# Attention and bit-weight feed-forward on one core: values ahead of scores on PE, another order of DMA issues, and the weight sums split over POOL and DVE

## The chip, the cores and the metric

The kernel runs on one core of one Trainium2 chip. The metric is the device time in microseconds (us) of one execution; the change is judged against the kernel before, timed on the same chip.

## The reference, cut to what matters

Inputs `x` and `ctx_2048` are [4, 1024, 1024] f32. The block is a causal cross attention with 16 heads of 64 columns (the context is both key and value), followed by a feed-forward whose weights are made from two four-bit-plane tensors of [1024, 1024, 4].

```python
q = heads(_layernorm(x)); k = v = heads(ctx)                    # 16 heads of 64
out = softmax(causal(q @ k.T * 64**-0.5)) @ v
x = x + out
soft = sigmoid(pweight) - sigmoid(nweight)                      # [1024, 1024, 4]
weight = einsum('oin,n->oi', soft, exps * sigmoid(mask_weight)) * scale
bias = round-to-4-bits(einsum('on,n->o', pbias - nbias, bexps)) * biasscale
x = x + _layernorm(x) @ weight.T + bias
```

## The kernel before, in words

**Tiles and jobs.** The 4 x 1024 rows make 32 tiles t of 128 rows; i = t % 8 is the place in the batch, so that tile t sees i+1 blocks of 128 keys. A tile's 16 heads are cut into jobs: 4 jobs of 4 heads for i = 0 and 1, 8 jobs of 2 heads for i = 2 and 3, and 16 jobs of one head for i = 4 to 7 ("16-step tiles"; q is the job's number in its tile). There are 352 jobs, and every engine walks through the same list, one step for each job j, with its own work of the step written out by hand. Nothing is scheduled by a planner: the order on each engine is the order of the code, and semaphores join the engines.

**One job on the five engines.** `scores(j)` (PE, L401, L402, L405) makes the scores of the job in one of two PSUM places (`slot`), as a sum of products in half precision, with the mask added by a last matmul. `maxima(j)` (DVE, L636) takes the row maxima, `exponentials(j)` (ACT, L520) writes exp to `p32`. `transpose_p(j)` (PE, L415) turns the 128 x 128 blocks of it into PSUM (`ptb`, two chunks), ACT writes the f16 high part (`high_parts`, L536) and DVE the f16 rest (`low_parts`, L642), and `values(j)` (PE, L434 and L436) multiplies both with the values into `oacc`. When four heads are done, ACT copies `oacc` to `osb` (`output`, L543), and POOL adds it to the row (`add_attention`, L867 to L876). PE fills each step with a piece of the feed-forward of an earlier tile (`linear`, L452).

**Turned jobs.** In tiles with one or two heads per job, jobs with q = 3, 6, 9, 12, 15 skip the transposes on PE. ACT writes the high part in place (L529, `p16`), DVE the low part (`low_part_unturned`, L650), and SP issues one DMA transpose (`turn_p`, L308) into `ptd`, from which `values(j)` reads. There are 92 such jobs.

**Distance.** In step j, PE does `scores` of job j+2, `values` of job j-2, the transposes of job j, and a piece of `linear`. DVE does in step j: `maxima(j+2)`, `low_part_unturned(j+1)` if job j+1 is turned, `low_parts(j)`, and the rest. So the scores of j+2 come in step j, the DMA transpose of j+1 is issued after it, and the values of j+1 are due three steps later.

**SP's list.** SP (SyncE) issues all DMAs in one written order: `turn_p`; `load_x` and `load_c` (rows and context of tile t+3); `turn_k`, `turn_q` (transposes of keys and queries of tile t+2, L296, L302); `swap_q` (two copies that make `qs`, L315, L316, which need `turn_q` landed); `turn_y`; `store`. A step number in SP's loop only sets the place in the list: SP goes on as soon as the semaphores that an issue waits for allow it.

**The weights.** Steps 0 to 15 (tiles 0 to 2) also make the feed-forward's weights, one unit u of two chunks w = 2u, 2u+1 per step: ACT takes tanh of both halves of each chunk (`chunk_tanh`, L582). For the even chunk DVE subtracts (L704), multiplies with the coefficients (L707) and sums over the four bits (L710); for the odd one POOL subtracts (`difference`, L883), and PE sums it with diagonal matrices (L475). PE turns both into `ffnb`, ACT (L576) and DVE (L715) split them into `wt`, and only then may PE begin the next unit.

## Time and profile before

| | us |
|---|---|
| median of three timed runs (1245.62 to 1248.9) | 1247.53 |
| the profiled execution's own time | 1242.35 |
| its span, first to last instruction | 1240.6 |
| PE busy in the span | 1114.4 (90%) |
| DVE busy | 1020.3 (82%) |
| ACT busy | 927.0 (75%) |
| POOL busy | 692.6 (56%) |

The granted TensorE clock is 0.975 of full speed over the span. PE's share is that of matmuls whose ends are modelled, and it averages over stages: up to about 170 us the weights are made beside the first jobs, then come the remaining tiles.

### The profile page before, as it was taken

How to read it: one execution, taken by the hardware profiler on the slowest of the kernel's cores; microseconds unless marked ns; L12 is line 12 of the kernel's file. 1: busy time of each engine (PE TensorE's matmuls, PEld its weight loads, DVE VectorE, ACT ScalarE, POOL GpSimd, SP SyncE). 2: the span in 40 equal slices, each digit the busy share in tenths (PEclk: the TensorE clock that was granted, in tenths of full speed). 3: DMA queues.
4: the chain of work that ended last, by engine and by line, in shares of the span. 5: the costliest groups of instructions: out<-in, count | busy, mean ns of one | idle time of the engine just before them, and what ended most of it. 6: DMA issues, size and time to landing. Idle time of an engine off the chain costs nothing. (4 is left out here: it accounts for less than half of the span.)

```text
span 1240.6 us, 28237 instructions
## 1 busy us (share of the span) xinstructions
PE 1114.4 (90%) x10820; PEld 813.7 (66%) x10820; DVE 1020.3 (82%) x1456; ACT 927.0 (75%) x1930; POOL 692.6 (56%) x766
## 2 busy tenths in 40 slices
PE   3687889989998999899998999899998998899988
PEld 2676756666766766666665777676776676676663
DVE  6989986888897887788897887888987887888862
ACT  5798975787887787777777787688787787787750
POOL 2456555554545886554445886554447986362351
PEclk8798999999999999999999999999999999999999
DMA  9699944756657888665667787576659886565442
GB/s 311 206 301 308 318 76 105 141 132 122 146 112 163 178 159 171 134 137 104 138 125 167 161 180 157 128 150 121 139 103 196 168 181 142 125 117 89 90 86 68
DMA packets 387189, 190.88 MB, mean 154 GB/s; under 512 B 358640, under 2 KB 358640, under 8 KB 387056
## 3 DMA queue, kind: packets, MB, share of 16 engines
q1 hardware_dynamic: 386048, 189.05, 67.7%
q8 instruction: 86, 1.41, 0.5%
q14 instruction: 47, 0.39, 0.1%
q10 hardware_dynamic: 1008, 0.04, 0.0%
HBM read 67.15 MB, written 16.78 MB: 68 GB/s over the span
## 5 line engine op out<-in xcount | busy, mean ns | idle before, releaser
L520 ACT ACTIVATE p<-slot,mx 128x512 f32<-128x512 f32 (+7 forms) x512 | 377.7, 746 | 151.7 <-DVE mx L636 94.2
L636 DVE TENSOR_REDUCE mx<-slot 128x1 f32<-128x640 f32 (+7 forms) x352 | 356.5, 1015 | 42.4 <-PE slot L405 40.5
L452 PE MATMUL ffnb<-wt,yt 128*128 128x512 f16 x1464 | 374.5, 382 | 3.1 <-DVE ring L698 1.7
L642 DVE SCALAR_TENSOR_TENSOR pt<-ptb,pt 128x512 f16<-128x512 f32 (+1 forms) x504 | 281.3, 598 | 100.4 <-ACT pt L536 100.3
L401 PE MATMUL slot<-kt,qt 128*128 128x128 f16 (+3 forms) x1056 | 269.5, 285 | 23.5 <-ACT p L520 11.3
L402 PE MATMUL slot<-kt,qs 128*128 128x128 f16 (+3 forms) x1056 | 268.8, 284 | 0.0
L536 ACT ACTIVATE pt<-ptb 128x512 f16<-128x512 f32 (+1 forms) x504 | 239.4, 527 | 31.9 <-PE ptb L415 30.7
L867 POOL TENSOR_TENSOR att<-osb 128x256 f32<-128x256 f32 x128 | 100.2, 783 | 289.2 <-ACT osb L543 282.8
L415 PE MATMUL ptb<-id,p 128*128 128x128 f32 x1700 | 240.3, 280 | 11.7 <-DVE pt L642 10.5
L452 PEld LDWEIGHTS ffnb<-wt,yt 128*128 128x128 f16 x1464 | 137.4, 99 | 104.3 <-issue 4.8
L434 PE MATMUL oacc<-v,pt 128*128 128x128 f16 x1700 | 180.4, 220 | 23.8 <-ACT osb L543 10.9
L415 PEld LDWEIGHTS ptb<-id,p 128*128 128x128 f32 x1700 | 182.1, 141 | 18.9 <-issue 15.9
L434 PEld LDWEIGHTS oacc<-v,pt 128*128 128x128 f16 x1700 | 150.4, 98 | 45.5 <-ACT osb L543 19.3
L436 PE MATMUL oacc<-v,pt 128*128 128x64 f16 x1700 | 173.0, 193 | 0.0
L401 PEld LDWEIGHTS slot<-kt,qt 128*128 128x128 f16 x1056 | 105.1, 100 | 100.9 <-ACT p L520 31.8
L650 DVE SCALAR_TENSOR_TENSOR p<-p 128x640 f16<-128x640 f32 (+3 forms) x92 | 138.4, 1505 | 19.7 <-ACT p L529 17.7
L436 PEld LDWEIGHTS oacc<-v,pt 128*128 128x128 f16 x1700 | 148.1, 98 | 0.1
L402 PEld LDWEIGHTS slot<-kt,qs 128*128 128x128 f16 x1056 | 104.3, 99 | 52.2 <-issue 0.7
L543 ACT ACTIVATE osb<-oacc 128x512 f32<-128x512 f32 x128 | 76.4, 597 | 53.3 <-PE oacc L436 53.0
L876 POOL TENSOR_TENSOR ring<-ring,att 128x256 f32<-128x256 f32 x128 | 105.6, 825 | 10.1
L405 PE MATMUL slot<-maskb,idb 128*128 128x128 bf16 x512 | 111.2, 221 | 0.0
L520 ACT ACTIVATION_READ_ACCUMULATOR p<-slot,mx 128x1 f32 x512 | 106.9, 209 | 0.0
(96 smaller groups left out, 1517.1 us busy)
## 6 DMA issues: line engine op xcount, KB each, us to landing
ring<-in_x_dram SPq DMA_DIRECT2D x32, 512.0 KB, 4.7
cin<-in_ctx_dram SPq DMA_DIRECT2D x32, 512.0 KB, 4.0
out_dram<-ring SPq DMA_DIRECT2D x32, 512.0 KB, 3.4
qs<-qt SPq DMA_DIRECT2D x124, 128.0 KB, 2.8
v<-in_L_ffn_pweight_dram SPq DMA_DIRECT2D x22, 512.0 KB, 6.7
kt<-in_L_ffn_nweight_dram SPq DMA_DIRECT2D x16, 512.0 KB, 7.6
v<-in_L_ffn_nweight_dram SPq DMA_DIRECT2D x6, 512.0 KB, 6.3
kt<-in_L_ffn_pweight_dram SPq DMA_DIRECT2D x5, 512.0 KB, 4.8
```

The costliest lines, as they stand in the source:

```text
L401: pe.matmul(dst, qt[:, t % 2, h, :], keys, start=True, stop=False, skip_group_check=True)
L402: last = pe.matmul(dst, qs[:, h, :], keys, start=False, stop=end <= i, skip_group_check=True)
L405: last = pe.matmul(slot[:, j.par, base + i * P:base + (i + 1) * P], idb[:, :], maskb[:, :], start=False, stop=True, skip_group_check=True)
L415: last = pe.transpose(ptb[:, c % 2, at * P:(at + 1) * P], p32[:, j.par, k * P:(k + 1) * P], id32[:, :])
L434: pe.matmul(oacc[:, h % GROUP, :], turned[:, k, :], v, start=blk == 0, stop=False, skip_group_check=True)
L436: last = pe.matmul(oacc[:, h % GROUP, 0:D], turned[:, j.blocks + k, :], v[:, 0:D], start=False, stop=blk == j.i, skip_group_check=True)
L452: last = pe.matmul(dst, yt[:, k % 2, a * KT_N + kk, :], wt[:, c, kk, half * 512:half * 512 + 512], start=r == 0, stop=r == 3 * KT_N - 1)
L520: last = nc.scalar.activation(p32[:, j.par, hh * j.keys:(hh + 1) * j.keys], slot[:, j.par, base:base + j.keys], ACT.Exp, bias=mx[:, j.par, ...
L536: nc.scalar.activation(pt[:, j.par, blocks.start:blocks.stop, :], ptb[:, c % 2, 0:P * len(blocks)].rearrange("p (k c) -> p k c", c=P), ACT ...
L636: nc.vector.tensor_reduce(mx[:, j.par, 0:j.heads], src[:, 0:j.heads, 0:j.keys], AX_X, ALU.max, negate=True).then_inc(mx_ready, 1)
L642: nc.vector.scalar_tensor_tensor(pt[:, j.par, j.blocks + blocks.start:j.blocks + blocks.stop, :], ptb[:, c % 2, 0:P * len(blocks)].rearran ...
L650: nc.vector.scalar_tensor_tensor(p16[:, size:2 * size], p32[:, j.par, 0:size], P_SCALE, p16[:, 0:size], ALU.mult, ALU.subtract).then_inc(p ...
```

## The change

1. On PE, `values` of the job two back stands ahead of `scores` of the job two on, in every step.
2. On SP, in 16-step tiles: `load_x` and `load_c` both at step 9 (they were at 8 and 7), `turn_k` at 12 (was 9), `turn_q` at 14, which is behind `turn_p(15)` as before, but ahead of `turn_k` in the last tile of a batch. `LOADS` leaves the other tiles as they were.
3. The sum over the four bits on DVE: one multiplication and three multiply-adds on 256 elements, each with a stride of four in its source, take the place of one multiplication and one reduction on 1024. The subtraction ahead of it goes to POOL for every second unit (`on_pool`).

```diff
+LOADS = {4: (2, 2), 8: (4, 4), 16: (9, 9)}
...
+def on_pool(w):
+    return w % 4 != 2
+def differences_to(w):
+    return sum(on_pool(v) for v in range(w + 1))
 def turn_k_step(t):
-    return 9 if steps(t) == 16 and t % NT < NT - 1 else steps(t) - 1
+    return 12 if steps(t) == 16 and t % NT < NT - 1 else steps(t) - 1
...
# SP
+                    if s == 14 and n == 16 and t + 2 < TILES:
+                        turn_q(t + 2)
-                    if s == n // 2 and t + 3 < TILES:
+                    if s == LOADS[n][0] and t + 3 < TILES:
                         load_x(t + 3)
-                    if s == C_LO[n] + n // 16 and t + 3 < TILES:
+                    if s == LOADS[n][1] and t + 3 < TILES:
                         load_c(t + 3)
...
-                    if s == n - 1 and t + 2 < TILES:
+                    if s == n - 1 and n < 16 and t + 2 < TILES:
                         turn_q(t + 2)
# PE
-                pe.wait_ge(d_ready, u + 1)
+                pe.wait_ge(d_ready, differences_to(2 * u + 1))
...
             for j in JOBS:
+                if j.n > 1:
+                    values(JOBS[j.n - 2])
                 if j.n + 2 < len(JOBS):
                     scores(JOBS[j.n + 2])
-                if j.n > 1:
-                    values(JOBS[j.n - 2])
                 transpose_p(j)
# DVE, weights_sum(u): before
-                dve.wait_ge(th_ready, w + 1)
-                nc.vector.tensor_tensor(pairs[w % PAIRS][0], pairs[w % PAIRS][0], pairs[w % PAIRS][1], ALU.subtract
-                                        ).then_inc(w_sub, 1)
-                nc.vector.tensor_tensor(a, a, coef.unsqueeze(1).to_broadcast([P, WCH, NBITS]), ALU.mult
-                                        ).then_inc(w_mul, 1)
-                nc.vector.tensor_reduce(pairs[w % PAIRS][1][:, 0:WCH], a, AX_X, ALU.add).then_inc(w_sum, 1)
# DVE, weights_sum(u): now
+                if u % 2:
+                    dve.wait_ge(th_ready, w + 1)
+                    nc.vector.tensor_tensor(d, d, c, ALU.subtract).then_inc(w_sub, 1)
+                    dve.wait_ge(w_sub, u // 2 + 1)
+                else:
+                    dve.wait_ge(d_ready, differences_to(w))
+                nc.vector.tensor_scalar(acc, bit[:, :, 0], coef[:, 0:1], None, ALU.mult).then_inc(w_mul, 1)
+                nc.vector.scalar_tensor_tensor(acc, bit[:, :, 1], coef[:, 1:2], acc, ALU.mult, ALU.add
+                                               ).then_inc(w_mul, 1)
...
# POOL
+                if j.n + 1 < UNITS and on_pool(2 * j.n + 2):
+                    difference(2 * j.n + 2)
                 if j.n > 1 and JOBS[j.n - 2].closes_group:
                     add_attention(JOBS[j.n - 2].group)
                 if j.n + 1 < UNITS:
-                    difference(j.n + 1)
+                    difference(2 * j.n + 3)
```

PE, tile 4 (one head, five key blocks), the first turned job, whose values read `ptd`. Before:

```order
L405 MATMUL slot<-maskb,idb 128x128
L434 MATMUL oacc<-v16,ptd 128x128
L436 MATMUL oacc<-v16,ptd 128x64
L434 MATMUL oacc<-v16,ptd 128x128
L436 MATMUL oacc<-v16,ptd 128x64
L434 MATMUL oacc<-v16,ptd 128x128
L436 MATMUL oacc<-v16,ptd 128x64
L434 MATMUL oacc<-v16,ptd 128x128
L436 MATMUL oacc<-v16,ptd 128x64
L434 MATMUL oacc<-v16,ptd 128x128
L436 MATMUL oacc<-v16,ptd 128x64
L415 MATMUL ptb<-id32,p32 128x128 x5
```

And of the change (L466 is `linear`, L448 and L450 `values`, L415 the scores with `kt16`):

```order
L466 MATMUL ffnb<-wt,yt 128x512 x4
L448 MATMUL oacc<-v16,ptd 128x128
L450 MATMUL oacc<-v16,ptd 128x64
L448 MATMUL oacc<-v16,ptd 128x128
L450 MATMUL oacc<-v16,ptd 128x64
L448 MATMUL oacc<-v16,ptd 128x128
L450 MATMUL oacc<-v16,ptd 128x64
L448 MATMUL oacc<-v16,ptd 128x128
L450 MATMUL oacc<-v16,ptd 128x64
L448 MATMUL oacc<-v16,ptd 128x128
L450 MATMUL oacc<-v16,ptd 128x64
L415 MATMUL slot<-kt16,qt 128x512
```

The values stood between the scores' last matmul and the transposes; they stand between `linear` and the scores' first matmul now.

SP, the last tile of a batch (tile 7), from `turn_p` of its job 6. Before:

```order
L308 DMA_TRANSPOSE ptd<-p 128x16x128
L315 DMA qs<-qt 64x1024
L316 DMA qs<-qt 64x1024
L283 DMA cin<-in_ctx_dram 128x1024
L308 DMA_TRANSPOSE ptd<-p 128x16x128
L279 DMA ring<-in_x_dram 128x1024
L308 DMA_TRANSPOSE ptd<-p 128x16x128
L315 DMA qs<-qt 64x1024
L316 DMA qs<-qt 64x1024
L308 DMA_TRANSPOSE ptd<-p 128x16x128
L296 DMA_TRANSPOSE kt<-v 128x16x128
L302 DMA_TRANSPOSE qt<-q 128x16x128
```

And of the change (L320 is `turn_p`, L291 `load_x`, L295 `load_c`, L314 `turn_q`, L308 `turn_k`, L327 and L328 `swap_q`):

```order
L320 DMA_TRANSPOSE ptd<-p 128x16x128
L327 DMA qs<-qt 64x1024
L328 DMA qs<-qt 64x1024
L320 DMA_TRANSPOSE ptd<-p 128x16x128
L291 DMA ring<-in_x_dram 128x1024
L295 DMA cin<-in_ctx_dram 128x1024
L320 DMA_TRANSPOSE ptd<-p 128x16x128
L327 DMA qs<-qt 64x1024
L328 DMA qs<-qt 64x1024
L320 DMA_TRANSPOSE ptd<-p 128x16x128
L314 DMA_TRANSPOSE qt<-q 128x16x128
L308 DMA_TRANSPOSE kt<-v 128x16x128
```

The context's load went from ahead of the second `turn_p` shown to behind it, and `turn_q` and `turn_k` changed places.

DVE, a unit of the weights whose subtraction goes to POOL (u = 6). Before:

```order
L642 SCALAR_TENSOR_TENSOR pt<-ptb,pt 128x512 [waits hi_done] x2
L704 TENSOR_TENSOR v16<-v16 128x1024 [waits w_tanh]
L707 TENSOR_TENSOR v16<-v16,small 128x1024 [waits w_sub]
L710 TENSOR_REDUCE v16<-v16 128x256 [waits w_mul]
L715 TENSOR_TENSOR wt<-ffnb,wt 128x4x128 [waits w_hi]
```

And of the change (L656 is `low_parts`, L739 `weights_low`; `w_diff` is POOL's semaphore `d_ready`):

```order
L656 SCALAR_TENSOR_TENSOR pt<-ptb,pt 128x512 [waits hi_done] x2
L725 TENSOR_SCALAR v16<-v16,small 128x256 [waits w_diff]
L727 SCALAR_TENSOR_TENSOR v16<-v16,small 128x256 [waits w_mul]
L730 SCALAR_TENSOR_TENSOR v16<-v16,small 128x256 [waits w_mul]
L733 SCALAR_TENSOR_TENSOR v16<-v16,small 128x256 [waits w_mul]
L739 TENSOR_TENSOR wt<-ffnb,wt 128x4x128 [waits w_hi]
```

Three instructions on 1024 elements gave way to four on 256, and the wait is for POOL's subtraction and not for ACT's tanh.

## Rows read from the trace of the kernel before

**Rows 1.** Busy time by stage: us, then PE, PEld, DVE, ACT, POOL, clock, DMA.
```profile
31.00:155.00 124.00, 94.35 (x635) 86.57 (x634) 114.54 (x139) 105.14 (x197) 68.54 (x56) 0.87 0.88 283
...
172.00:1216.00 1044.00, 975.60 (x9897) 697.60 (x9896) 868.18 (x1270) 793.69 (x1684) 607.53 (x678) 0.99 0.67 137
```

**Rows 2.** PE's waits, 172 to 1216 us: who for whom, us, times, longest.
```profile
PE oacc L434 <- DMA ptd<-p: 16.1, 15, 2.3
...
PE slot L401 <- issue: 9.8, 3, 3.8
PE oacc L434 <- DVE pt L642: 9.4, 15, 1.3
```

**Rows 3.** Timeline of tile 21 (six key blocks), a turned job: start, us, engine.
```profile
816.48 0.27 PE L401 MATMUL slot<-kt,qt 128*128 128x256 f16 x1
817.05 2.13 POOL L848 TENSOR_TENSOR v<-cin,v 128x1024 f16<-128x1024 f32 x1
817.19 0.22 PE L434 MATMUL oacc<-v,ptd 128*128 128x128 f16 x1
817.70 0.85 PE L415 MATMUL ptb<-id,p 128*128 128x128 f32 x6
817.82 0.95 DVE L636 TENSOR_REDUCE mx<-slot 128x1 f32<-128x768 f32 x1
818.69 1.31 DVE L650 SCALAR_TENSOR_TENSOR p<-p 128x768 f16<-128x768 f32 x1
820.02 1.72 SPq L308 DMA_TRANSPOSE ptd<-p  x1
824.63 0.23 PE L434 MATMUL oacc<-v,ptd 128*128 128x128 f16 x1 [0.29 <-DMA ptd<-p]
```

**Rows 4.** All DMA transposes of turned jobs (L308), by source line.
```profile
DMA to landing us min/median/max: 3.3/4.3/6.1
```

**Rows 5.** Stretches of tiles 20, 21, 22 and 23, columns as in rows 1.
```profile
747.32:788.29 40.97, 37.03 (x410) 28.47 (x408) 32.55 (x57) 29.71 (x68) 26.34 (x28) 1.00 0.72 152
788.29:830.91 42.62, 39.02 (x411) 29.81 (x411) 36.00 (x56) 33.33 (x69) 22.43 (x25) 1.00 0.68 136
830.91:876.04 45.13, 42.26 (x453) 32.45 (x452) 39.02 (x56) 36.01 (x67) 22.24 (x25) 1.00 0.69 133
876.04:924.57 48.53, 47.06 (x496) 34.80 (x494) 44.34 (x55) 38.22 (x65) 20.69 (x24) 1.00 0.59 116
```

**Rows 6.** DVE by form and by source line: count, busy us, mean ns; or min/median/max.
```profile
L636 DVE TENSOR_REDUCE mx<-slot 128x1 f32<-128x1024 f32 x64 | 77.1, 1209 | 2.0 <-PE slot L405 1.6
L642 DVE SCALAR_TENSOR_TENSOR pt<-ptb,pt 128x256 f16<-128x256 f32 x44 | 18.2, 413 | 0.0
L650 DVE SCALAR_TENSOR_TENSOR p<-p x92: 824/1226/2756, 212.7 to 1197.2; 128x768 f16<-128x768 f32 x26, 128x1024 f16<-128x1024 f32 x26, 128x640 f16<-128x640 f32 x20, 128x896 f16<-128x896 f32 x20
```

**Rows 7.** Timeline of SP and PE as batch 1 begins (tile 9's scores at 393.73).
```profile
382.57 3.66 SPq L296 DMA_TRANSPOSE kt<-v  x1
386.33 2.23 SPq L302 DMA_TRANSPOSE qt<-q  x1
390.72 0.46 SPq L315 DMA_DIRECT2D qs<-qt  x1
...
393.73 0.22 PE L401 MATMUL slot<-kt,qt 128*128 128x128 f16 x1 [3.00 <-issue]
```

**Rows 8.** DVE and POOL in the weights' stage, timeline; two stretches.
```profile
43.05 2.36 POOL L883 TENSOR_TENSOR v<-v,yt 128x1024 f32<-128x1024 f32 x1 [6.01 <-ACT yt L582]
43.38 2.08 DVE L727 TENSOR_TENSOR y<-y 128x32 f32<-128x32 f32 x1
...
80.49 1.37 DVE L704 TENSOR_TENSOR v<-v 128x1024 f32<-128x1024 f32 x1
81.89 1.23 DVE L707 TENSOR_TENSOR v<-v,small 128x1024 f32<-128x1024 f32 x1
83.15 1.22 DVE L710 TENSOR_REDUCE v<-v 128x256 f32<-128x1024 f32 x1
```

More of the change, by code:

```diff
@@ L701, in weights_sum @@
                 w = 2 * u
-                a = pairs[w % PAIRS][0].rearrange("p (k n) -> p k n", n=NBITS)
-                dve.wait_ge(th_ready, w + 1)
-                nc.vector.tensor_tensor(pairs[w % PAIRS][0], pairs[w % PAIRS][0], pairs[w % PAIRS][1], ALU.subtract
-                                        ).then_inc(w_sub, 1)
-                dve.wait_ge(w_sub, u + 1)
-                nc.vector.tensor_tensor(a, a, coef.unsqueeze(1).to_broadcast([P, WCH, NBITS]), ALU.mult
-                                        ).then_inc(w_mul, 1)
-                dve.wait_ge(w_mul, u + 1)
-                nc.vector.tensor_reduce(pairs[w % PAIRS][1][:, 0:WCH], a, AX_X, ALU.add).then_inc(w_sum, 1)
+                d, c = pairs[w % PAIRS]
+                if u % 2:
[4 more added lines that the diff above has]
+                    dve.wait_ge(d_ready, differences_to(w))
+                bit = d.rearrange("p (k n) -> p k n", n=NBITS)
+                acc = c[:, 0:WCH]
+                nc.vector.tensor_scalar(acc, bit[:, :, 0], coef[:, 0:1], None, ALU.mult).then_inc(w_mul, 1)
+                dve.wait_ge(w_mul, 3 * u + 1)
+                nc.vector.scalar_tensor_tensor(acc, bit[:, :, 1], coef[:, 1:2], acc, ALU.mult, ALU.add
+                                               ).then_inc(w_mul, 1)
+                dve.wait_ge(w_mul, 3 * u + 2)
+                nc.vector.scalar_tensor_tensor(acc, bit[:, :, 2], coef[:, 2:3], acc, ALU.mult, ALU.add
+                                               ).then_inc(w_mul, 1)
+                dve.wait_ge(w_mul, 3 * u + 3)
+                nc.vector.scalar_tensor_tensor(acc, bit[:, :, 3], coef[:, 3:4], acc, ALU.mult, ALU.add
+                                               ).then_inc(w_sum, 1)
             def weights_low(u):
@@ L877, in add_attention, with difference @@
                                         ).then_inc(x1_ready, 1)
-            def difference(u):
-                w = 2 * u + 1
+            def difference(w):
                 pool.wait_ge(th_ready, w + 1)
@@ L900, in _ @@
             difference(0)
+            difference(1)
             made, q_made = 0, 2
```

## The prediction

> **What bounds the kernel now.** I read the busy time by stage first [rows 1]. From 172 to 1216 us PE is busy 975.6 of 1044 us (93%), DVE 83%, ACT 76%: PE is the bound of this stage, and a stall of PE there costs its full length unless it takes the place of another. Before it, from 31 to 155 us, DVE is the fullest (114.5 of 124 us), ACT comes next (105.1) and PE has 94.4. That is the stage in which the weights are made; it is bound by DVE, with ACT close behind, and PE waits there.
>
> Then PE's waits in the long stage [rows 2]. The largest is for `ptd`, the DMA transpose of a turned job: 16.1 us in 15 waits. 92 jobs are turned, so most come in time now; the question is by how much. The timeline of one such job shows it [rows 3]. In one step of tile 21, PE starts the scores of job j+2 at 816.48, the values of the turned job before at 817.19, the transposes at 817.70. DVE takes the maxima of these scores from 817.82 to 818.77, then the low part of turned job j+1, 818.69 to 820.00 (it began while POOL's subtraction of 817.05 to 819.18 ran), SP issues its transpose at 820.02, and PE begins the values of j+1 at 824.63, after a wait of 0.29 us for it. From the scores' last matmul to these values the way is full: maxima, low part, DMA.
>
> **The change on PE.** It removes and adds no instruction on PE; it exchanges two blocks. Take `transpose_p(j)` and `linear` as fixed. The scores end later by the length of the values: 817.70 - 817.19 = 0.51 us with six blocks [rows 3]. The values are due earlier by the length of the scores: 817.19 - 816.48 = 0.71 us. So the way "scores of j+2 end, maxima, low part of j+1, DMA, values of j+1" has 0.51 + 0.71 = 1.22 us less. What stands on it after the change is a loop: the values of the last turned job (0.51), the scores (0.71, and 0.15 till the last matmul ends), maxima 0.95, low part 1.23 (the median [rows 6]), issue to landing 4.3 (the median [rows 4]), and about 0.2 for four handovers (an estimate; from DVE's end to SP's start it is 0.02 [rows 3]), together 8.05 us; then the next turned job's values, and so round. The loop spans three steps. Three steps of tile 21 take 42.62 x 3/16 = 7.99 us now [rows 5]. The same sum for the other widths (values and scores by 0.085 and 0.11 us per block, an estimate from the six-block lengths; maxima 0.8 to 1.21 [rows 6]) gives 7.7 for tile 20, 8.4 for 22 and 8.8 for 23, against 7.68, 8.46 and 9.10 now. So with median durations the loop is as long as PE's own work: half of the loops will be longer than it. A late loop costs PE its lateness, an early one gives nothing back, as PE can't run ahead of its own work. The low part lies between 0.82 and 2.76 us, the landing between 3.3 and 6.1: I take a spread of 0.8 us (one standard deviation) around a mean excess near 0.1. The mean of the positive part of that is 0.37 us, and 92 turned jobs make **+34 us**. Both ends: 0.12 us per job if the late low parts are late for POOL's sake and not for the scores' (then they don't move), +11; 0.6 if also the low parts of the turned-on-PE jobs come late, +55. For those speaks that PE waits 9.4 us in 15 waits for `pt` already [rows 2], and that DVE now does the maxima at the same time as PE the transposes, ahead of `low_parts`. What the exchange gives: the values cover a late exp at the step's start. That wait is below the ones shown in rows 2, under 9.4 us in all, and is inside the lengths that I compared with.
>
> **The change on SP.** In the last tile of a batch, `turn_k` (3.66 us to issue) stands ahead of `turn_q`, `turn_q` is issued at 386.33, and `swap_q`, which needs it landed, at 390.72; PE then waits 3.0 us with the first scores of tile 9, to 393.73 [rows 7]. Three batches do this, 9.8 us in all [rows 2]. With `turn_q` first it starts 3.66 us sooner; `swap_q` then stands behind `turn_k`'s issue, at about 382.6 + 2.2 + 3.7 = 388.5, which is 2.2 us sooner: **-7 us** over three batches (ends: -10, the whole wait, and 0, if the keys' transpose, now last, is the one missed). `load_c` no longer goes out just ahead of `turn_p(9)`. In tile 21, where it did, the transpose at 820.02 had not landed for the values at 824.63, 4.6 us later [rows 3]. I give 0.3 us to each of 16 such jobs, **-5 us** (ends 0 and -11). `turn_k` now follows `turn_p(12)` in place of `turn_p(9)`; both have a step or more till the next turn_p, and tile t+2's keys are due a tile later, so I cost it at nothing. Were SP late behind it, the turned job 15 would pay up to its 3.66 us of issue.
>
> **The change in the weights' stage.** DVE gives up for each unit a multiplication (1.23) and a reduction (1.22), and for eight of sixteen units a subtraction (1.37) [rows 8]. It gets one multiplication and three multiply-adds on 256 elements. Their price isn't in the trace; the nearest row is a multiply-subtract on 256 elements out of PSUM, 0.41 us [rows 6]. Bounds: 0.3 us (it scales down from 0.82 for 640 elements) and 1.2, if each waits for one POOL instruction. With 0.41 a sum is 1.65 and not 2.45 us: 16 x 0.8 + 8 x 1.37 = 24 us less for DVE. But ACT is busy 105.1 of the 124 us [rows 1] and has none of its work taken, so no more than 18.9 us can come out, and the chain "PE makes the unit, ACT and DVE split it, PE begins the next" stays. The moved subtraction takes 2.36 us on POOL for 1.37, DVE waits for it with `weights_low` and `maxima` queued behind, and POOL does `add_attention` after it. I take **-8 us** (ends 0 and -18.9).
>
> Here a rule speaks against the change. The row: a subtraction of 32 elements on DVE (L727) took 2.08 us, from 43.38 to 45.46, as long as POOL's subtraction of 43.05 to 45.41 ran [rows 8]. DVE's instructions with two SBUF sources wait for POOL's. The Trainium skill ("SBUF — State Buffer", Who interferes with whom) states this as a lock that is held for the whole instruction; by that rule, the trace agrees. Each multiply-add has two SBUF sources, and POOL gets eight more subtractions, so each sum may stand behind one; that is why I take less than half of the 18.9 us.
>
> The Trainium skill ("Vector Engine (DVE) Microarchitecture Reference", Points that are easy to get wrong) also says that this form of instruction runs at half rate with two SBUF sources that aren't bf16. The row L650 has f32 and f16 sources, and its 640 elements took 0.82 us at best [rows 6], 1.29 ns each, as little as the subtraction on 1024 elements with its 1.34 ns [rows 8]. That is the second rival below.
>
> **Sum.** +34 - 7 - 5 - 8 = +14 us on the profiled execution's 1242.35, 1256.4. That execution is 5.2 us under the median of the timed runs, so I forecast 1261.5, say **1262 us**.
>
> **Rivals.**
> 1. *The transposes are hidden anyway; the change is faster.* Place: the values of turned jobs. For it: only 15 of 92 wait now, and in many loops DVE reaches the low part late because of POOL, not because of the scores, so that 0.51 of the 1.22 us doesn't count. Against: tile 21's rows show nothing spare. With 0.12 us per job (+11), -7 - 5 - 12 beside it: -13, 1234 us. It decides from 0.22 us per turned job down, where +20 meets the three gains of 20. Chance 0.15.
> 2. *Multiply-adds at half rate.* Each takes 0.53 + 0.15 and not 0.41, 48 of them +13 us of DVE's 24 saved; with the wait for POOL's subtraction the stage gives nothing: +22, 1270. Chance 0.05; the row speaks against it.
> 3. *Two waits add up.* In the step after a turned job there are no transposes, so the low parts of the job ahead of it are due first, and turned values after them. If both slip, each loop is longer by the 1.22 us less what is spare, about 0.75: +69 - 12 - 8 = +49, 1297. For it: `pt` waits of rows 2. Chance 0.13.
> 4. *It cancels:* loss and gains each near 20, no change. Chance 0.09.
> My forecast's case has 0.58.
>
> **Numbers.** About 0.3% (3.7 us) is what a measurement of this kernel can tell from no change. The range takes the forecast's case from +20 to +45 for PE (1241 with gains of 26, 1280 with 12), rival 2, and half of rival 3; it leaves out most of rival 1: 1241 to 1290. Faster 0.17 (rival 1 and a little of the forecast's case), same 0.10, slower 0.73.
>
> **What would show it.** Right: PE's wait for `ptd` grows from 16 us to 40 or more, in over 40 waits; three steps of tile 20 and 21 become longer by 0.3 to 0.6 us; the wait of PE at the first scores of tiles 9, 17, 25 shrinks from 3.3 to about 1; L704 counts 8; the last unit of the weights is done some 8 us sooner; the new multiply-adds last 0.35 to 0.5 us apart from those that stand behind POOL. DVE's wait for ACT's `pt` falls, since maxima fill that time. Wrong: no more waits for `ptd` than now would take down the main term; multiply-adds of 0.7 us the third; the weights' stage not shorter, with ACT or POOL waiting in DVE's place, the same.

## The result and the profile after

The changed kernel takes 1276.07 us (median of four runs, 1274.9 to 1276.88) against 1246.74 of four runs of the kernel before beside it: ratio **1.0245**, 95% interval 1.0217 to 1.0273. It is slower, by 30 us. Here and below, each ratio is to the kernel before, timed beside the run on the same chip, with its 95% interval in brackets; differences are (ratio - 1) x 1246 us, and the interval of one is 1.5 to 5 us to either side. The texts on record write some of them as differences of the medians (+31.5 for +32.6, -15.4 for -15.0, +10.7 for +11.1). The lines of code named here moved by 12 to 24: L448 and L450 are the values, L415 and L416 the scores, L557 the copy of the finished group on ACT (`osb`), L650 the maxima, L656 `low_parts`, L664 the low part for a DMA transpose, L906 POOL's subtraction, L725, L727, L730 and L733 the new sum.

Busy time by stage, columns as in [rows 1]:

```profile
31.00:155.00 124.00, 86.49 (x557) 79.98 (x556) 106.53 (x143) 95.98 (x178) 75.03 (x57) 0.83 0.83 261
188.00:1250.00 1062.00, 966.35 (x9900) 683.87 (x9901) 871.05 (x1272) 796.70 (x1685) 604.51 (x678) 1.00 0.64 135
```

PE did less of its work in the first 124 us (557 matmuls where 635 were), and the long stage needs 1062 us for the matmuls that took 1044. The net loss of the two profiled executions has two places of about equal size. The last unit of the weights shows the first: `weights_low` (L739) of unit 16 starts at 183.5 us, and it started at 166.7 before.

```profile
L739 DVE TENSOR_TENSOR wt<-ffnb,wt x16: 636/677/692, 38.3 to 183.5; 128x512 f16<-128x512 f32 x16
```

PE's waits in the long stage, 188 to 1250 us, after:

```profile
PE oacc L448 <- ACT osb L557: 35.2, 42, 2.2
PE oacc L448 <- DVE pt L656: 31.3, 33, 1.6
PE oacc L448 <- DMA ptd<-p: 18.8, 29, 2.4
PE ptb L429 <- DVE pt L656: 5.5, 14, 2.1
PE slot L415 <- DMA qs<-qt: 1.4, 1, 1.4
```

and three rows of the same view of the kernel before (172 to 1216 us) that did not stand in [rows 2]:

```profile
PE oacc L434 <- ACT osb L543: 10.9, 21, 0.9
PE ptb L415 <- DVE pt L642: 10.5, 22, 2.0
...
PE slot L401 <- ACT p L520: 5.6, 15, 0.6
```

Three waits stand at the first matmul of the values. Together they were 36.4 us (16.1 and 9.4 of [rows 2], and 10.9) and are 85.3. The wait for the DMA transpose, on which the prediction built, grew least: 16.1 us in 15 waits to 18.8 in 29. What fell are the waits at the scores, 9.8 us at the batches' starts to under 2 and the one for exp, 5.6 us in 15 waits, to none, and the wait at the transposes (`ptb`), 10.5 us to 5.5.

Tiles 20, 21 and 22, to be read against [rows 5]:

```profile
769.94:809.76 39.82, 36.39 (x406) 27.64 (x404) 31.24 (x57) 30.78 (x69) 27.16 (x30) 1.00 0.70 148
809.76:854.49 44.73, 38.51 (x416) 29.17 (x414) 36.88 (x56) 32.50 (x67) 21.20 (x25) 1.00 0.59 126
854.49:903.09 48.60, 42.55 (x458) 31.74 (x456) 40.48 (x55) 36.04 (x67) 21.25 (x25) 1.00 0.63 123
```

Tile 20 became 1.2 us shorter, tiles 21 and 22 longer by 2.1 and 3.5: three steps of tile 21 take 8.39 us instead of 7.99.

Tile 21's turned job after, timeline (start, us, engine), to be read against [rows 3]:

```profile
838.94 0.96 DVE L650 TENSOR_REDUCE mx<-slot 128x1 f32<-128x768 f32 x1 [0.25 <-PE slot L419]
839.81 0.95 DVE L664 SCALAR_TENSOR_TENSOR p<-p 128x768 f16<-128x768 f32 x1
840.79 1.43 SPq L320 DMA_TRANSPOSE ptd<-p  x1
840.97 1.05 ACT L566 CAST q<-norm 128x1024 f16<-128x1024 f32 x1
841.90 0.61 ACT L557 ACTIVATE osb<-oacc 128x512 f32<-128x512 f32 x1
842.57 0.23 PE L448 MATMUL oacc<-v,pt 128*128 128x128 f16 x1 [0.49 <-ACT osb L557]
845.11 0.22 PE L448 MATMUL oacc<-v,ptd 128*128 128x128 f16 x1
```

The way from the maxima's start to the turned values is 6.17 us (838.94 to 845.11); it was 6.81 (817.82 to 824.63), and this transpose is in time, since the values one job ahead of it already stood for 0.49 us until ACT had copied `oacc`. ACT's list had a cast of 1.05 us ahead of that copy. DVE in turn waits for PE's scores more, 121.7 us in 139 waits of the long stage where it was 40.5 in 55.

One unit of the weights after, its subtraction now on POOL, timeline, to be read against [rows 8]:

```profile
83.42 2.35 POOL L906 TENSOR_TENSOR v<-v 128x1024 f32<-128x1024 f32 x1 [5.56 <-ACT v L596]
85.81 0.92 DVE L725 TENSOR_SCALAR v<-v,small 128x256 f32<-128x256 f32 x1 [3.63 <-POOL v L906]
86.77 0.84 DVE L727 SCALAR_TENSOR_TENSOR v<-v,small 128x256 f32<-128x256 f32 x1
87.64 0.90 DVE L730 SCALAR_TENSOR_TENSOR v<-v,small 128x256 f32<-128x256 f32 x1
88.11 2.60 POOL L906 TENSOR_TENSOR v<-v,kt 128x1024 f32<-128x1024 f32 x1
88.58 2.53 DVE L733 SCALAR_TENSOR_TENSOR v<-v,small 128x256 f32<-128x256 f32 x1
91.03 0.67 DVE L739 TENSOR_TENSOR wt<-ffnb,wt 128x512 f16<-128x512 f32 x1
```

DVE stands 3.63 us for POOL's subtraction, its multiply-adds take 0.84 and 0.90 us, and the last one, issued 0.47 us after POOL's next subtraction, takes 2.53. It ends at 91.11, 0.40 us behind POOL's subtraction (90.71), 1.9 us later than its own work would; `weights_low`, for which PE waits, is queued behind. Min/median/max of the last of the new lines in the `v` chunks (six of its sixteen instructions), where the median already is a wait for POOL:

```profile
L733 DVE SCALAR_TENSOR_TENSOR v<-v,small x6: 671/2516/2542, 29.8 to 173.8; 128x256 f32<-128x256 f32 x6
```

### The profile page after: what moved, and what is told of

Same layout as the page of the kernel before. It is cut to its first block, busy times and chain, and to the rows that moved or that the text cites. A ratio compares the mean times of both kernels' runs of the same rounds, so it can differ in the third digit from the quotient of the medians.

```text
span 1274.9 us, 28269 instructions
## 1 busy us (share of the span) xinstructions
PE 1110.3 (87%) x10820; PEld 804.9 (63%) x10820; DVE 1029.5 (81%) x1480; ACT 930.1 (73%) x1930; POOL 708.9 (56%) x774
## 4 chain that ended last, share of the span: by engine, by line
PE 37%; DVE 25%; DMA 14%; ACT 10%; issue 7%; POOL 6%; SPq 0%; POOLq 0%; ACTq 0%
DMA ptd<-p 13%; PE ffnb L466 11%; DVE p L664 8%; DVE mx L650 5%; PE oacc L448 5%; PE ptb L429 5%; PE slot L415 5%; PE slot L416 5%; DVE pt L656 4%; DVE stats L677 2%; ACT p L534 2%; PE oacc L450 2%; ACT pt L550 2%; POOL norm L849 2%; ACT osb L557 2%
## 5 line engine op out<-in xcount | busy, mean ns | idle before, releaser
L650 DVE TENSOR_REDUCE mx<-slot 128x1 f32<-128x640 f32 (+7 forms) x352 | 358.4, 1018 | 126.2 <-PE slot L419 124.5
L466 PE MATMUL ffnb<-wt,yt 128*128 128x512 f16 x1464 | 372.8, 381 | 2.0 <-DVE ring L712 1.1
L656 DVE SCALAR_TENSOR_TENSOR pt<-ptb,pt 128x512 f16<-128x512 f32 (+1 forms) x504 | 281.0, 597 | 48.4 <-ACT pt L550 45.9
L415 PE MATMUL slot<-kt,qt 128*128 128x128 f16 (+3 forms) x1056 | 270.5, 286 | 9.9 <-ACT p L534 6.2
L416 PE MATMUL slot<-kt,qs 128*128 128x128 f16 (+3 forms) x1056 | 270.1, 285 | 0.0
L448 PE MATMUL oacc<-v,pt 128*128 128x128 f16 x1700 | 184.2, 223 | 72.6 <-ACT osb L557 35.2
L429 PE MATMUL ptb<-id,p 128*128 128x128 f32 x1700 | 233.8, 276 | 5.6 <-DVE pt L656 5.5
L448 PEld LDWEIGHTS oacc<-v,pt 128*128 128x128 f16 x1700 | 152.9, 100 | 133.1 <-ACT osb L557 61.6
L466 PEld LDWEIGHTS ffnb<-wt,yt 128*128 128x128 f16 x1464 | 139.6, 98 | 105.5 <-issue 2.5
L450 PE MATMUL oacc<-v,pt 128*128 128x64 f16 x1700 | 176.2, 195 | 0.0
L450 PEld LDWEIGHTS oacc<-v,pt 128*128 128x128 f16 x1700 | 150.2, 99 | 18.0 <-issue 0.3
L664 DVE SCALAR_TENSOR_TENSOR p<-p 128x640 f16<-128x640 f32 (+3 forms) x92 | 138.3, 1503 | 4.7 <-ACT p L543 3.1
L415 PEld LDWEIGHTS slot<-kt,qt 128*128 128x128 f16 x1056 | 103.6, 99 | 33.6 <-ACT p L534 6.4
L416 PEld LDWEIGHTS slot<-kt,qs 128*128 128x128 f16 x1056 | 104.6, 99 | 18.9 <-issue 0.3
L894 POOL TENSOR_TENSOR att<-att,rinv 128x256 f32<-128x256 f32 x128 | 85.6, 669 | 24.6 <-DVE rinv L671 15.4
```

The lines of the kernel that those rows point to most:

```text
L415: pe.matmul(dst, qt[:, t % 2, h, :], keys, start=True, stop=False, skip_group_check=True)
L416: last = pe.matmul(dst, qs[:, h, :], keys, start=False, stop=end <= i, skip_group_check=True)
L429: last = pe.transpose(ptb[:, c % 2, at * P:(at + 1) * P], p32[:, j.par, k * P:(k + 1) * P], id32[:, :])
L448: pe.matmul(oacc[:, h % GROUP, :], turned[:, k, :], v, start=blk == 0, stop=False, skip_group_check=True)
L450: last = pe.matmul(oacc[:, h % GROUP, 0:D], turned[:, j.blocks + k, :], v[:, 0:D], start=False, stop=blk == j.i, skip_group_check=True)
L466: last = pe.matmul(dst, yt[:, k % 2, a * KT_N + kk, :], wt[:, c, kk, half * 512:half * 512 + 512], start=r == 0, stop=r == 3 * KT_N - 1)
```

## The experiments

### The three parts, one at a time

**TensorE's order alone.** The kernel before with these lines:

```diff
+                if j.n > 1:
+                    values(JOBS[j.n - 2])
                 if j.n + 2 < len(JOBS):
                     scores(JOBS[j.n + 2])
-                if j.n > 1:
-                    values(JOBS[j.n - 2])
```

> The kernel before with only PE's order changed (values of the job two back ahead of the scores). Theory A (the values are due earlier while ACT's, DVE's and SP's queues stay tied to the transposes, so all three waits at the values grow): +17 to +27 us, PE's waits at the values near 85 us in sum against 36, and the wait of the scores for exp gone. Rival B (the whole loss is from the weights' stage): within 5 us of before.

1.0262 (1.0233 to 1.0290), +32.6 us: above Theory A's +17 to +27, with the waits that it named, 90.5 us at the values, and none left for exp. Its waits at the values, 176 to 1250 us:

```profile
PE oacc L434 <- ACT osb L543: 35.1, 43, 2.2
PE oacc L434 <- DVE pt L642: 31.5, 35, 1.6
PE oacc L434 <- DMA ptd<-p: 23.9, 27, 2.3
```

**SyncE's order alone.** `LOADS`, `turn_k` at 12, `turn_q` at 14 as in the diff of the change, nothing else.

> The kernel before with only SP's list changed. Forecast's terms: -7 us where batches begin and -5 us for the turned job 9, so -12. If the gain is only where batches begin: -5 to -7, with the three waits of PE at the first scores of tiles 9, 17 and 25 (9.8 us) down to under 3.

0.9880 (0.9847 to 0.9913), -15.0 us: faster than both kernels, and near the -12. The three waits at the batches' starts fell from 9.8 to 4.4 us, not to under 3.

**The weights' part alone.** The sums and the subtractions as changed, both lists as before.

> The kernel before with only the weight sums changed (the multiply-adds, and every second subtraction on POOL). Theory A (multiply-adds at 0.68 us and standing behind POOL's subtraction make the stage longer by themselves): +10 to +17 us, all of it before tile 3. Rival B (they lose only together with PE's new order): within 4 us of before. The forecast had -8.

1.0089 (1.0058 to 1.0119), +11.1 us, inside Theory A's range. The last unit starts 11.8 us later.

The three add to +28.7 us against +30.5 measured together, the same within their intervals. Two more kernels take one part back out of the changed one. **The changed kernel with the old sums and subtractions:**

> The changed kernel with the weights' part undone: SyncE's and TensorE's orders as changed, sums and subtractions as before. If the parts add (+31.5 - 15.4): +16 us against before, about 1.013; if the orders of the two lists feed each other, under +10 or over +22. The prediction's own sum without its -8 was +22.

1.0169 (1.0138 to 1.0199), +21.1, above the +16 and short of the 22 that would have spoken for a feedback. **The changed kernel with PE's old order** (the diff above, reversed):

> The changed kernel with TensorE's order undone. If the parts add (-15.4 + 10.7): -5 us against before, about 0.996.

0.9979 (0.9967 to 0.9991), -2.6. So in the changed kernel the weights' part costs 30.5 - 21.1 = 9.4 us, PE's order 33.1, and SP's order, from +32.6 to +21.1, gives back 11.5 where it gave 15.0 alone. Each of these carries an interval of 3 to 5 us, so 11.5 and 15.0 can't be told apart, nor 9.4 and 11.1.

### The weights: which part, and why

**The sums alone**, all even subtractions on DVE as before (shortened; the last line stands for three, n = 1, 2, 3):

```diff
-    nc.vector.tensor_tensor(a, a, coef..., ALU.mult)
-    nc.vector.tensor_reduce(pairs[w % PAIRS][1][:, 0:WCH], a, AX_X, ALU.add)
+    nc.vector.tensor_scalar(acc, bit[:, :, 0], coef[:, 0:1], None, ALU.mult)
+    nc.vector.scalar_tensor_tensor(acc, bit[:, :, n], coef[:, n:n + 1], acc, ALU.mult, ALU.add)
```

> The kernel before with one edit: each sum of four on VectorE is one TENSOR_SCALAR and three multiply-adds instead of a product over 1,024 and a reduction; all its subtractions stay on VectorE. The product and reduction of before take 1.26 + 1.31 = 2.57 us a unit; the four new ones should take, by the trace of the changed kernel, 0.47 + 3 x 0.69 = 2.54 us with GpSimd idle, and about 2.2 to 2.5 us for each that stands behind a subtraction on GpSimd. Theory (the multiply-adds save nothing and queue behind GpSimd): the same or slower, +0 to +8 us against before. Rival (they save time and the moved subtraction is what costs the +10.7 us of the weights' part alone): -4 to -10 us.

1.0119 (1.0082 to 1.0157), +14.8 us, more than either answer gave, and the opposite of the rival's saving. **The moved subtraction alone**, product and reduction as before:

```diff
+    if u % 2:
         nc.vector.tensor_tensor(d, d, c, ALU.subtract)
+    else:
+        dve.wait_ge(d_ready, differences_to(w))
```

> The kernel before with one edit: GpSimd also takes the even subtraction of every second unit; product and reduction as before. Theory A (the multiply-adds are what costs): the subtraction moved saves VectorE 1.26 us in 16 units and costs GpSimd 2.35 us each, -3 to +3 us against before. Theory B (GpSimd's longer queue, with VectorE's sums waiting for it, costs most of the +10.7 us): +6 to +11 us.

1.0021 (1.0007 to 1.0035), +2.6 us: Theory A's answer, at its upper end. DVE's sixteen sums with their subtractions, added up over their lines in the traces: 63.7 us before, 54.5 with the subtraction moved, 95.1 with the new sums, 82.5 with both, 79.3 in the changed kernel. The new sum, not the move, is what costs. At their shortest in these traces old and new sum take the same: 1.22 + 1.22 = 2.44 us, and 0.45 + 0.67 + 0.68 + 0.67 = 2.46. In the run with the sums alone 27 of the 64 new instructions began while an instruction of POOL ran; these 27 took 32.7 us more than their shortest, the other 37 together 0.5 us more. In the changed kernel it is 33 of 64, with 29.3 us, and 0.4 us for the rest. So it is POOL, and hardly anything else, that makes the new sums long; how much of DVE's longer list reaches the end (31.4 us on DVE, 14.8 in the time) is not followed further. The moved work came back as a wait, 7.1 + 5.9 + 3.7 us (31 to 188 us of that run; one row):

```profile
DVE v L722 <- POOL v L897: 7.1, 2, 3.6
```

**The forms by themselves**, six of each on DVE alone, first with POOL idle; no part of the reference is computed:

> No part of the reference's work: DVE alone does six of each form on f32 and f16 data, first with POOL idle, then with POOL in a chain of subtractions on 1024 elements. Theory A (a multiply-add with two f32 SBUF sources runs at half rate, whatever the stride): 256 elements 0.68 us with stride 4, contiguous, and with an immediate; 1024 elements 2.3 us; 0.41 us if one source is f16 or in PSUM. Rival B (the stride of four costs it): contiguous 0.41 us, stride 4 0.68 us, and the same for an addition with stride 4. With POOL busy, forms with two SBUF sources take up to 2.4 us more, the reduction nothing.

The timeline's rows (start, us of all six): L68 multiply-add over 256 with stride 4, L70 contiguous, L78 its first source in PSUM, L80 over 1024, L84 an addition over 1024, L86 and L88 TENSOR_SCALAR with stride 4 and contiguous.

```profile
11.13 4.17 DVE L68 SCALAR_TENSOR_TENSOR acc<-four,coef,acc 128x256 f32<-128x256 f32 x6
15.33 3.09 DVE L70 SCALAR_TENSOR_TENSOR acc<-four,coef,acc 128x256 f32<-128x256 f32 x6
...
28.54 3.08 DVE L78 SCALAR_TENSOR_TENSOR acc<-bank,coef,acc 128x256 f32<-128x256 f32 x6
31.65 7.89 DVE L80 SCALAR_TENSOR_TENSOR acc<-four,coef,acc 128x1024 f32<-128x1024 f32 x6
...
43.41 7.53 DVE L84 TENSOR_TENSOR acc<-four,acc 128x1024 f32<-128x1024 f32 x6
50.97 2.85 DVE L86 TENSOR_SCALAR acc<-four,coef 128x256 f32<-128x256 f32 x6
53.86 2.29 DVE L88 TENSOR_SCALAR acc<-four,coef 128x256 f32<-128x256 f32 x6
```

The stride of four f32 makes 0.515 us, with the handover to the next instruction, into 0.695, which is what the rival said of the stride. Two f32 sources in SBUF cost nothing beside one in PSUM (3.09 and 3.08), and 1024 elements take 1.31 us, 5% more than the addition: no half rate, and Theory A is out.

**The same forms while POOL runs 90 subtractions**, line numbers one higher:

> Forms of VectorE alone, six of each, while GpSimd runs a chain of subtractions over 1,024; nothing of the reference is computed. With GpSimd idle they took 0.695 us (multiply-add over 256, stride 4), 0.475 (TENSOR_SCALAR, stride 4), 0.38 (contiguous), 0.633 (addition, stride 4), 1.255 (addition over 1,024), 1.315 (multiply-add over 1,024), 1.25 (reduction). If only forms with two sources in SBUF wait for a whole instruction of GpSimd: TENSOR_SCALAR and the reduction keep their time, the additions rise above 2 us. If TENSOR_SCALAR waits too (two of four stood at 2.5 us in some units of the run with four of them): it rises to about 2.4 us.

```profile
L81 DVE SCALAR_TENSOR_TENSOR acc<-four,coef,acc 128x1024 f32<-128x1024 f32 x6 | 18.8, 3128 | 0.2
...
L71 DVE SCALAR_TENSOR_TENSOR acc<-four,coef,acc 128x256 f32<-128x256 f32 x6 | 14.6, 2436 | 0.2
L87 DVE TENSOR_SCALAR acc<-four,coef 128x256 f32<-128x256 f32 x6 | 14.5, 2413 | 0.2
...
L91 DVE TENSOR_REDUCE acc<-four 128x256 f32<-128x1024 f32 x6 | 7.3, 1220 | 0.2
L79 DVE SCALAR_TENSOR_TENSOR acc<-bank,coef,acc 128x256 f32<-128x256 f32 x6 | 2.9, 484 | 0.2
...
L94 DVE COPY res<-src 128x4 f32<-128x4 f32 x1 | 2.2, 2185 | 0.0
```

TENSOR_SCALAR waits too, so the second answer of the expectation holds: each such instruction of 256 elements or fewer takes about as long as one subtraction of POOL (a copy of four elements 2.19 us). The reduction and the form that reads PSUM don't wait. So the old sum had one instruction that could stand behind POOL, its product; the reduction, 1.22 us in all sixteen, could not. The new one has four. POOL waits as well: its subtraction takes 2.34 us once DVE is idle, 2.43 beside the multiply-adds on 256 elements and 3.20 beside the forms on 1024.

**Stride or lock?** The sums alone with contiguous sources, so that other columns are summed:

```diff
-    nc.vector.scalar_tensor_tensor(acc, bit[:, :, 1], coef[:, 1:2], acc, ALU.mult, ALU.add)
+    nc.vector.scalar_tensor_tensor(acc, d[:, 256:512], coef[:, 1:2], acc, ALU.mult, ALU.add)
```

> The sums alone in multiply-adds (all even subtractions on VectorE; +14.8 us against before), with one edit: each multiply-add reads 256 neighbouring elements instead of every fourth, so the sums are of other columns and the output is not the reference's. Theory S (the stride of 16 bytes is most of the price: 0.695 against 0.515 us a multiply-add with GpSimd idle): 48 multiply-adds save 0.18 us each, 8.6 us of VectorE, and the time falls to about +6 against before. Theory L (most of it is the wait for a whole instruction of GpSimd, which the contiguous form has too, 2.2 to 2.5 us each): VectorE's time in the 48 multiply-adds stays over 45 us and the time stays at +10 to +15.

1.0011 (0.9995 to 1.0028), +1.4 us: more came back than the 8.6 us of theory S. DVE's time fell from 95.1 to 75.3 us, of which about 10 is the stride (48 multiply-adds at 0.18 and 16 TENSOR_SCALAR at 0.10); for the rest the shorter instructions met POOL less often. Fifteen of the 48 multiply-adds took over 2 us with the stride, ten without it. Both theories had a part, and neither had the size.

**Four TENSOR_SCALAR, the additions left out:**

```diff
-    nc.vector.scalar_tensor_tensor(acc, bit[:, :, 1], coef[:, 1:2], acc, ALU.mult, ALU.add)
+    nc.vector.tensor_scalar(acc, bit[:, :, 1], coef[:, 1:2], None, ALU.mult)
```

> As the sums alone, but all four instructions of a sum are TENSOR_SCALAR with one tensor as source: the additions of the other three products are left out, and the output is not the reference's. Theory L (it is the form with two sources in SBUF that waits for GpSimd): nearly all four run at 0.47 to 0.8 us, VectorE spends about 33 us in them instead of 72, and the kernel is faster than before by 3 to 10 us. Rival (four instructions with waits between them are dear in any form): still +5 or more.

1.0022 (1.0006 to 1.0038), +2.7 us. Theory L's forecast fell: DVE spends 54.8 us in the four, not 33, and the kernel is not faster than before. Eleven of the 64 took over 2 us, which the run with POOL busy then explained.

### TensorE's order: which wait

**The old order where the values open a group** (they wait for `osb`):

```diff
+                late = j.n > 1 and JOBS[j.n - 2].opens_group
+                if j.n > 1 and not late:
                     values(JOBS[j.n - 2])
                 if j.n + 2 < len(JOBS):
                     scores(JOBS[j.n + 2])
+                if late:
+                    values(JOBS[j.n - 2])
```

> The order of TensorE's list alone as in the run with only that part (+31.5 us against before), but the old order (scores first) in the jobs whose values open a group, that is, wait for the output's copy on ScalarE. Theory (three waits at the values share the loss by where each job's last condition comes; about 35 of 85 us of them at the group openers): 8 to 14 us of the 31.5 come back, so +18 to +24 against before. Rival (the loop through the transposes' DMA alone, as the prediction had it): openers are not special; a quarter to a half of the jobs go back at their share of 3 us or so: +27 to +31.

1.0167 (1.0139 to 1.0194), +20.8 us, the theory's answer: 11.8 us came back. **The old order where they are turned** (`late` is `JOBS[j.n - 2].d is not None`):

> The order of TensorE's list alone, but the old order in the jobs whose values use transposes made by DMA. By the prediction's theory (the lateness sits at those 92 jobs and no other): all of the loss comes back, +0 to +5 us against before. By the theory that output copy, low part and transposes share it by how early the values come: about half comes back, +12 to +22.

1.0096 (1.0066 to 1.0125), +12.0 us: not the 0 to 5 of the prediction's theory, but the lower end of the other. **The new order there only** (`late` is `... is None`):

> TensorE's new order only where the values come from a transpose by DMA (92 jobs); the complement of the run with the old order there, which was +12 of the +31.5 us. If the loss adds up by job: +17 to +21 us against before. If the two kinds of job feed each other (a late opener makes the next turned job late): under +15.

1.0239 (1.0213 to 1.0265), +29.8 us: above what either answer gave. The two halves, 12.0 and 29.8, are more than the whole, 32.6. PE's waits, turned jobs only first, then all but the turned (176 to 1270 and 176 to 1250 us):

```profile
PE oacc L434 <- DMA ptd<-p: 45.8, 45, 3.4
...
PE oacc L434 <- DVE pt L645: 10.4, 19, 1.3
...
PE oacc L434 <- ACT osb L546: 7.4, 12, 1.6
```

```profile
PE oacc L434 <- ACT osb L546: 40.0, 45, 1.9
PE oacc L434 <- DVE pt L645: 25.7, 28, 1.6
PE oacc L434 <- DMA ptd<-p: 10.4, 10, 2.4
```

With the group openers kept in the old order, the transposes' wait is 33.6 us in 28, more than with all moved. With the turned values alone moved, the wait is the predicted one, 45.8 us in 45 waits. Where the others are moved as well, a wait for `osb` or `pt` comes ahead of it in the same three steps, and the transposes have landed by then. The traces bear this out: 45 turned values waited with the turned alone moved; with all moved 22 of these 45 no longer wait for their transpose, and at 21 of the 22 PE had waited for `osb` or `pt` since the turned job before. The loss is much the same (+29.8 and +32.6), the name on it changes.

**The low part ahead of the maxima on DVE**, with PE's new order:

```diff
+                if j.n + 1 < len(JOBS) and JOBS[j.n + 1].d is not None:
+                    low_part_unturned(JOBS[j.n + 1])
                 if j.n + 2 < len(JOBS):
                     maxima(JOBS[j.n + 2])
-                if j.n + 1 < len(JOBS) and JOBS[j.n + 1].d is not None:
-                    low_part_unturned(JOBS[j.n + 1])
```

> TensorE's new order alone (+31.5 us), and on VectorE the low part for the next transpose by DMA goes ahead of the maxima of the job two on. If the loop of the prediction (values late, scores late, maxima late, low part late, DMA late) is what costs at these 92 jobs: the transposes start up to 1.0 us sooner, the waits for them fall from 24 to under 10 us, and 8 to 18 us come back (+14 to +24 against before). If the exponentials behind the maxima matter as much: the maxima are 0.6 us later and nothing comes back (+28 to +36).

1.0642 (1.0619 to 1.0664), +80.0 us, far outside both. PE's waits and one of DVE's:

```profile
PE oacc L434 <- ACT osb L543: 71.0, 50, 2.8
PE oacc L434 <- DVE pt L642: 49.3, 44, 2.4
...
PE oacc L434 <- DMA ptd<-p: 2.0, 6, 0.6
```

```profile
DVE p L650 <- ACT p L529: 90.4, 87, 1.6
```

The wait for the transpose is gone, as meant. But at 87 of 92 turned jobs DVE now stands for ACT's copy of exp with the maxima behind it, so exp comes later (ACT waits 139.4 us for the maxima, where it waited 110.6 with PE's order alone). By these waits the branch scores, maxima, exp, copy of `oacc` has no more room than the one through the DMA; no run separates the two further.

### SyncE's order: the two terms

**`turn_q` at step 14 alone:**

```diff
+                    if s == 14 and n == 16 and t + 2 < TILES:
+                        turn_q(t + 2)
-                    if s == n - 1 and t + 2 < TILES:
+                    if s == n - 1 and n < 16 and t + 2 < TILES:
```

> Of SyncE's new order one part alone: in tiles of 16 steps the transpose of the next query tile goes at step 14, ahead of that of the keys in a batch's last tile, instead of at step 15. The prediction priced it at -7 us (0 to -10). If it is most of the -15.4 us of the whole order: -8 to -11.

0.9950 (0.9931 to 0.9968), -6.2 us, less than the -8 to -11 of a part that is most of the whole. **The loads at 9 and `turn_k` at 12 alone:**

```diff
-    return 9 if steps(t) == 16 and t % NT < NT - 1 else steps(t) - 1
+    return 12 if steps(t) == 16 and t % NT < NT - 1 else steps(t) - 1
-                    if s == n // 2 and t + 3 < TILES:
+                    if s == LOADS[n][0] and t + 3 < TILES:
```

> The other part alone: in tiles of 16 steps the loads of x and of the context both at step 9 (8 and 7 before), and the transpose of the keys at step 12 instead of 9. The prediction priced it at -5 us (0 to -11). If the two parts share the -15.4 us: -4 to -8.

0.9946 (0.9926 to 0.9965), -6.7 us. One wait of PE answers to each, 171 to 1216 us; `turn_q` first, then the loads:

```profile
PE slot L403 <- DMA qs<-qt: 4.2, 3, 1.5
```

```profile
PE oacc L435 <- DMA ptd<-p: 9.8, 10, 2.4
```

The first was 9.8 us, the second 16.1 [rows 2]: 5.6 and 6.3 us less, which is what the runs gained. The second is `load_c`, by where the waits lie: of the fifteen for `ptd` before, seven with 7.8 of the 16.1 us are at jobs with q = 9, whose transpose `load_c` went out just ahead of. One of these is left with the loads at 9, 0.7 us, while the waits of the other jobs stay, 8.3 us in 8 before and 9.1 in 9 after. `turn_k` did not stand ahead of `turn_p(9)` in either order.

**SyncE's order, and in the weights' stage the low parts of queries and context on POOL:**

```diff
 def low_on_pool(t):
-    return t > 3 and steps(t) > 4
+    return steps(t) > 4
```

> The whole new order of SyncE's list (-15.4 us alone) and one edit more: in the tiles of 8 steps of the first four, the low parts of queries, context and the normed sum are made on GpSimd instead of on VectorE. VectorE was busy for 142 of 157 us in the weights' stage and TensorE waited 28 us for it there; six such subtractions of 2.1 to 2.6 us go. If VectorE's list bounds that stage: 5 to 12 us sooner, 1219 to 1226 us. If they come late from GpSimd (84.7 us of 157 busy) or hold up VectorE's additions: 1230 to 1240.

0.9896 (0.9873 to 0.9918), against 0.9880 (0.9847 to 0.9913) without the edit: no difference that these runs can tell, and not the 5 to 12 us of the first answer. DVE has 7 us less to do from 31 to 188 us (134.4 for 141.5), and PE did not get on faster by that much. Either of the two is the best version here, 13 to 15 us faster than the kernel before.

## Why the prediction was wrong

It forecast +14 us and had the direction; 30 was measured, inside its range only because that allowed for a PE term of up to +45. The step that failed is the weights' term (3). Term by term:

1. **PE, +34: right in size, mostly right in place, half right in the wait.** Alone it is +32.6, in the changed kernel 33.1. The exchange costs its time at the turned jobs: with only these 92 exchanged it is +29.8, 0.32 us per job where 0.37 was taken. The jobs that are not turned, which the sum put at nothing, cost 12.0 us when they alone are exchanged, and most of that hides behind the turned ones when all are; that the whole comes so near to +34 is in part luck. Nor is the lateness one spread around a common mean: in the run with the turned alone 36 of the 45 waits are at q = 3, 9 and 12. "PE's wait for `ptd` grows from 16 us to 40 or more, in over 40 waits" is what the run with them alone shows (45.8 in 45). In the changed kernel it does not (18.8 in 29), because the step left out the copy of `oacc` by ACT and gave `pt` a place in its upper end alone: the values come earlier, by about the scores' 0.71 us, for every one of their conditions. The text named the fall of `ptd` waits as what would take the main term down; that test was wrong, since the same loss passes under two other names. Tile 22 grew by 0.65 us per three steps, tile 21 by 0.40, tile 20 not at all, where 0.3 to 0.6 was said of tiles 20 and 21.

2. **SP, -7 and -5: right.** -6.2 and -6.7 alone, each with the wait that the term named. Together they are -15.0. Beside PE's new order it is 11.5, which the intervals don't tell from 15.0; in the traces the batches' starts then give back 5.0 us (6.6 to 1.6) where they give 5.4 alone (9.8 to 4.4), so nothing there shows a gain lost.

3. **The weights, -8: the step that failed.** It is +11.1 alone and +9.4 in the changed kernel, an error of 17 to 19 us, which is all of the miss: the sum without it is +22, and the changed kernel without that part measures +21.1. Two things went wrong in it. The price of a multiply-add was taken as 0.41 us, from a form that reads PSUM without a stride. At its best it is 0.67 with the stride, near the 0.7 that the text named as a sign of being wrong, and over the 48 of the changed kernel the lines L727, L730 and L733 add up to 57.6 us, 1.20 each: the text's own upper bound of 1.2, "if each waits for one POOL instruction". The second is that this bound was not carried into the ends of the term: with 1.2 a sum is 4.0 and not 2.45 us, sixteen of them 25 us more, 14 after the eight subtractions. The ends should have been -18.9 and +14, not 0. A form that waits for POOL was foreseen, one wait a sum; what was missed is that one long instruction of two became four short ones, each of which can find POOL ahead of it, and that the reduction it replaced did not wait in any of its sixteen (1.22 us each).

4. **The rule on the shared port was the right one to weigh.** The Trainium skill ("SBUF — State Buffer", Who interferes with whom) says that an instruction with two SBUF inputs, and copies and `tensor_scalar` in their two-port modes, exclude GpSimd's, while a reduction never does. This case's trace agrees in each: 2.44, 2.19, 2.41, and 1.22 us unchanged; which mode an instruction ran in it doesn't tell. The prediction used only its first half. The same page (Door 1, the note on cachelines) says that each access to a new line of 16 bytes is penalised; the trace agrees, 0.695 against 0.515 us with a stride of 16 bytes, and that would have spoken against 0.41. The note goes on to call a stride of up to four f32 free; these runs differ, since four f32 is the stride that was measured.

5. **Rival 2, half rate,** gave +22 us for another reason than what happened: over 1024 contiguous elements the form takes 1.31 us beside the addition's 1.25. The rule of the Trainium skill that it rests on ("Vector Engine (DVE) Microarchitecture Reference", Points that are easy to get wrong) is not what these runs measure. Rival 3 (+49) is out, for PE's order is +33. Rival 1 is out.

6. **Other marks.** The subtractions on DVE are eight, as foreseen. At the batches' starts two waits are left, 1.4 and 0.3 us, in place of three of 3.3, "to about 1" as said. DVE's wait for ACT's `pt` in the long stage fell from 98.4 to 45.2 us, as said. The last unit of the weights was to be done 8 us sooner and is 16.8 later. Of this 13.5 is the weights' part (183.5 against 170.0 us with the old sums); the other 3.3 is no more than the scatter between traces, for SP's order, which changes nothing in tiles 0 to 2, moves it by 3.5.

## What to carry to other kernels

Price a replaced instruction by its form, its stride and its neighbour: where two engines exclude each other, count how often the new sequence can be caught, not only how long each piece is. Carry the bound of every unknown price through to the ends of its term, also past zero. When a consumer is moved earlier in an engine's list, look at each of its conditions; the one that ends last gets the name of the loss, and the wait's name in a profile is no measure of which condition is tight.

## What was not expected of the hardware

A TENSOR_SCALAR over 256 f32 with one tensor source took 0.475 us, handover included, with GpSimd idle and 2.41 while GpSimd subtracted, a COPY of 4 elements 2.19; a multiply-add whose tensor source is in PSUM kept its 0.48, a reduction its 1.22. Both engines pay, the one with short instructions far more: GpSimd's subtraction took 2.34 us with VectorE idle, 2.43 beside multiply-adds on 256 elements, which went from 0.48 to 2.44, and 3.20 beside the forms on 1024 elements, which went from 1.31 and 1.25 to 3.13 and 3.24.
